# Cross-attention chain on one core: the front put in another order, with work moved between engines

## The reference, cut to what matters

```python
def L0(tgt, memory, Wq, Wk, Wv):
    q, k, v = heads(tgt @ Wq.T), heads(memory @ Wk.T), heads(memory @ Wv.T)   # 16 heads of 16
    att = softmax(q @ k.T / 4) @ v
    return tgt + att[0]
def L1(X, F):                      # X = ctx, F = L0's result
    nX, nF = layernorm(X, w1, b1), layernorm(F, w2, b2)
    attended = softmax(nF @ nX.T / 16) @ nX
    ca = gelu(attended @ fc1.T + fc1_b) @ fc2.T + fc2_b        # fc1: 256 -> 4, fc2: 4 -> 256
    nc = layernorm(ca, w3, b3)
    return nF + gamma2 * (ca + gamma1 * (softmax(nc @ nc.T / 16) @ nc))
```

## Time and profile before

| | us |
|---|---|
| median of 3 runs (lowest, highest) | 247.23 (247.22, 247.85) |
| the profiled execution's own time | 246.86 |
| its span, first to last instruction | 245.1 |
| busy: PE, DVE, ACT, POOL | 214.2, 198.0, 148.9, 124.4 |

### The profile page before, as it was taken

The page is one execution under the profiler, slowest core; times in us unless marked ns, Lnnn a source line. Parts: engine busy times, 40 slices in busy tenths (PEclk is TensorE's granted clock), DMA queues, the critical chain, the costliest instruction groups (busy, mean ns, idle before and its releaser), DMA issues.

```text
span 245.1 us, 4980 instructions
## 1 busy us (share of the span) xinstructions
PE 214.2 (87%) x1758; PEld 154.2 (63%) x1758; DVE 198.0 (81%) x391; ACT 148.9 (61%) x284; POOL 124.4 (51%) x184
## 2 busy tenths in 40 slices
PE   6989989677999999999999899999978569999750
PEld 6766548446878779697787787867645225554320
DVE  6888858899999978789899999733558958998764
ACT  2167856226778678596787968846775326666310
POOL 6000096776999999969698939200002522222220
PEclk9999999999999999999999999999999759999955
DMA  6990000242455514455243000000000022444566
GB/s 186 366 350 3 1 4 0 93 143 109 173 171 148 161 56 155 174 168 174 82 151 113 3 1 3 0 1 3 0 3 1 0 88 86 173 175 174 190 238 257
DMA packets 14712, 26.81 MB, mean 109 GB/s; under 512 B 1760, under 2 KB 1760, under 8 KB 14688
## 3 DMA queue, kind: packets, MB, share of 16 engines
q1 hardware_dynamic: 14688, 26.50, 31.2%
HBM read 18.11 MB, written 8.39 MB: 108 GB/s over the span
## 4 chain that ended last, share of the span: by engine, by line
PE 55%; DVE 28%; issue 8%; ACT 4%; POOL 2%; DVEq 0%; POOLq 0%; ACTq 0%
PE psum L981 15%; PE psum L918 7%; DVE bn L381 6%; DVE xN L401 6%; PE psum L989 5%; PE psum L873 5%; DVE nm L564 3%; PE psum L1019 3%; PE psum L1095 3%; PE psum L931 2%; DVE nmax L524 2%; PE psum L1001 2%; PE psum L946 2%; PE psum L959 2%; PE psum L888 2%
## 5 line engine op out<-in xcount | busy, mean ns | idle before, releaser
L981 PE MATMUL psum<-XT,Fall 128*128 128x256 f32 x256 | 60.9, 381 | 1.8 <-ACT Fall L763 1.8
L981 PEld LDWEIGHTS psum<-XT,Fall 128*128 128x128 f32 x256 | 46.1, 190 | 7.2 <-ACT Fall L763 2.2
L656 POOL TENSOR_SCALAR cN<-cN,nmean,rstd 128x256 f32<-128x256 f32 x64 | 38.5, 614 | 2.4 <-POOL rstd L643 2.3
L636 POOL TENSOR_TENSOR xN<-xN,tgt 128x512 f32<-128x512 f32 x28 | 35.7, 1278 | 1.6 <-DVE xN L401 1.6
L401 DVE TENSOR_SCALAR xN<-xN,bn,rstd 128x256 f32<-128x256 f32 x64 | 33.8, 571 | 0.7 <-POOL rstd L643 0.7
L786 ACT ACTIVATE PT<-psum 128x512 f32<-128x512 f32 x32 | 19.2, 599 | 24.3 <-PE psum L989 24.2
L700 POOL CAST sC<-co 128x160 bf16<-128x160 f32 x8 | 2.6, 322 | 61.6 <-DVE co L581 61.6
L793 ACT ACTIVATE E<-psum,nmax 128x256 f32<-128x256 f32 x64 | 26.8, 475 | 10.9 <-DVE nmax L524 10.9
L524 DVE TENSOR_REDUCE nmax<-psum 128x2 f32<-128x512 f32 x32 | 22.0, 686 | 13.7 <-PE psum L981 13.2
L643 POOL TENSOR_TENSOR rstd<-vps,minus_half 128x8 f32<-128x8 f32 (+1 forms) x16 | 25.0, 1564 | 15.4 <-DVE vps L392 15.3
L760 ACT ACTIVATE XT<-psum,b1s,w1s 128x512 f32<-128x512 f32 x32 | 23.1, 794 | 3.8 <-PE psum L918 3.8
(11 more groups left out here) (157 smaller groups left out, 348.5 us busy)
## 6 DMA issues: line engine op xcount, KB each, us to landing
cN<-ctx SPq DMA_DIRECT2D x32, 256.0 KB, 2.9
xN<-x SPq DMA_DIRECT2D x32, 256.0 KB, 4.2
out<-Fall SPq DMA_DIRECT2D x32, 256.0 KB, 2.3
x0T<-x0t SPq DMA_DIRECT2D x1, 256.0 KB, 2.6
wqT<-wqt SPq DMA_DIRECT2D x1, 256.0 KB, 2.9
c0T<-c0t SPq DMA_DIRECT2D x1, 256.0 KB, 3.7
wkT<-wkt SPq DMA_DIRECT2D x1, 256.0 KB, 4.8
wvT<-wvt SPq DMA_DIRECT2D x1, 256.0 KB, 5.0
```

Source lines behind the costliest of these rows:

```text
L636: pool.tensor_tensor(xN[:, b % SLOTS, :], xN[:, b % SLOTS, :], tgt2[:, :, :].rearrange("p t d -> p (t d)"), ALU.add).then_inc(y_ok, 1)
L656: pool.tensor_scalar(own, own, nmean[:, p % 4, NT * m + t:NT * m + t + 1], root_of(p, 0, m, t), ALU.add, ALU.mult)\
L981: last = pe.matmul(bank[SBANK1[b % 3]][:, t * N:(t + 1) * N], Fall[:, b, c, t * P:(t + 1) * P], XT[:, p % 4, c, m * N:(m + 1) * N], start= ...
```

## The change

It does these things, all ahead of or at the start of the loop:

- Transfers: `c0T` and `wkT` are issued by ACT, at its very start. SP issues `x0T`, `wqT`, `wvT`, then eight ctx tiles, then eight x tiles (before: two and two).
- PE's start: 3 dummy products, the mean, 2 dummy products (before: 7, then the mean).
- The keys are projected in two halves with a signal after each, into two banks, and masked half by half on DVE. The scores of the first two heads wait for the first half's two masks.
- The order behind the keys: first scores, `operand_products`, second scores, first value half, first transposes, third scores, second value half (before: products, first value half, scores, second value half, a wait for ACT's value copies, second scores).
- `output_operand` leaves DVE. POOL does the same in 17 instructions with a wait on each, after its memsets and once the algebra's `prods` are there.
- Means and variances of the first ctx tiles are made by pair (`first_variances`), and POOL takes the root and normalizes by pair. The statistics of the sixth ctx tile move behind DVE's last copy of the attention.
- All six first x tiles are added by DVE. Their normalization moves from DVE to ACT: DVE makes `shift0` = -mean/deviation, and ACT applies it with the deviation's inverse as scale (four instructions for each pair).
- `project(0)`, ACT's copy and `project_back(0)` stand before the first turn of x, with 3 and 6 dummy products around (before: 11 dummy products there, and `project(0)` in the loop).

The core of the diff:

```diff
@@ sync
-        for dst, src, arrived in ((x0T, x0t, q_in), (wqT, wqt, q_in), (c0T, c0t, k_in), (wkT, wkt, k_in),
-                                  (wvT, wvt, v_in)):
+        for dst, src, arrived in ((x0T, x0t, q_in), (wqT, wqt, q_in), (wvT, wvt, v_in)):
             sp.dma_start(dst[:, :, :], src).then_inc(arrived, 16)
...
+        for src, dst, arrived in ((c_d, cN, c_in), (x_d, xN, x_in)):
+            for b in range(SLOTS):
+                sp.dma_start(dst[:, b, :], src[b, :, :]).then_inc(arrived[b], 16)
@@ vector
-        output_operand(0)
-        dve.wait_ge(k_mm, 1)
-        for e, m in enumerate(("even", "odd")):
-            dve.tensor_scalar(kTm[:, e, :, :], tiles(bank[1]), c_(m), None, ALU.mult).then_inc(kT_ok, 1)
...
-        output_operand(1)
+        def masked(o):
+            dve.wait_ge(k_mm, o + 1)
+            for e, m in enumerate(("even", "odd")):
+                dve.tensor_scalar(kTm[:, e, o, :], bank[(1, 5)[o]][:, 0:N], c_(m), None, ALU.mult).then_inc(kT_ok, 1)
+        masked(0)
+        masked(1)
...
+        def first_variances(p):
+            dve.wait_ge(st_ok, 2 * p + 2)
...
+                if p in (1, 3):
+                    first_variances(p // 2)
...
         dve.tensor_copy(oT[:, 1, :], bank[1][:, :]).then_inc(oT_ok[1], 1)
+        statistics(2 * EARLY - 1, 0)
+        first_variances(EARLY - 1)
...
+        def shifts(p):
+            dve.wait_ge(root_ok, p + 1)
+            dve.scalar_tensor_tensor(shift0[:, p, :].rearrange("p (m t) -> p m t", t=NT),
+                                     bn[:, p, 1, :, :].rearrange("p m (t k) -> p m t k", t=NT)[:, :, :, 1], -1.0,
+                                     rstd[:, p, 1, :].rearrange("p (m t) -> p m t", t=NT), ALU.mult, ALU.mult)\
+                .then_inc(shift0_ok, 1)
+        for p in range(EARLY):
+            add(2 * p)
+            add(2 * p + 1)
+            if p >= 1:
+                shifts(p - 1)
+            statistics(2 * p, 1)
+            statistics(2 * p + 1, 1)
+            variances(p)
...
-            if b == 18:
-                output_operand(2)
@@ gpsimd
+        pool.wait_ge(alg, ALG["prods"])
+        step(pool.tensor_tensor(g12[:, :], c_("g1"), c_("g2"), ALU.mult))
+        for c in range(DC):
+            step(pool.tensor_scalar(Rt[:, c, 0:H], a5[:, c, 0:H], c_("g2", c), None, ALU.mult))
...
+        for p in range(EARLY):
+            pool.wait_ge(vps_first, 2 * p + 2)
+            pool.tensor_tensor(rstd[:, p, 0, :], vps[:, p, 0, :], minus_half[:, 0:2 * NT], ALU.pow).then_inc(root_first, 1)
+            normal(2 * p)
+            normal(2 * p + 1)
         root(0)
-        add(4)
         root(1)
-        add(5)
@@ scalar
+        for dst, src in ((c0T, c0t), (wkT, wkt)):
+            act.dma_start(dst[:, :, :], src).then_inc(k_in, 16)
...
+        evacuate(0, 0)
+        evacuate(1, 0)
+        turned_values(0)
+        evacuate(2, 0)
+        normal(0)
+        normal(1)
         evacuate(0, 1)
+        normal(2)
+        normal(3)
...
             exponentials(b)
+            if b < 2:
+                normal(b + 4)
@@ tensor
-        keep_busy(7, 4)
+        keep_busy(3, 4)
...
+        keep_busy(2, 4)
...
-        keep_busy(11, 7)
...
+        project(0)
+        keep_busy(3, 7)
+        project_back(0)
+        keep_busy(6, 7)
         turned(0, 1)
```

More of the change, by code:

```diff
@@ L548, in _ @@
             maximum(b)
+            if b == 0:
+                shifts(EARLY - 1)
             if b % 4 == 2:
@@ L800, in turned, with normal @@
             act.activation(sT[:, p % 2, :], bank[4][:, 0:NT * P].bitcast(BF16), ACT.Copy).then_inc(sT_ok[p % 2], 1)
-        for p in range(EARLY):
-            evacuate(p, 0)
+        def normal(b):
+            p, m = b // 2, b % 2
+            act.wait_ge(shift0_ok, p + 1)
+            for t in range(NT):
+                own = xN[:, b, t * D:(t + 1) * D]
+                act.activation(own, own, ACT.Identity, bias=shift0[:, p, NT * m + t:NT * m + t + 1],
+                               scale=root_of(p, 1, m, t)).then_inc(first_ok, 1)
+        evacuate(0, 0)
[4 more added lines that the diff above has]
+        normal(1)
         evacuate(0, 1)
+        normal(2)
+        normal(3)
         for b in range(B):
@@ L882, in _ @@
         last.then_inc(mean_mm, 1)
[L884 to L890 removed]
+        keep_busy(2, 4)
+        pe.wait_ge(q_in, 32)
+        for o in range(2):
+            for c in range(DC):
+                last = pe.matmul(bank[0][:, o * N:(o + 1) * N], wqT[:, c, o * P:(o + 1) * P], x0T[:, c, :],
+                                 start=c == 0, stop=c == DC - 1)
+        last.then_inc(q_mm, 1)
+        pe.wait_ge(k_in, 32)
+        for o in range(2):
+            for c in range(DC):
+                last = pe.matmul(bank[(1, 5)[o]][:, 0:N], wkT[:, c, o * P:(o + 1) * P], c0T[:, c, :],
+                                 start=c == 0, stop=c == DC - 1)
+            last.then_inc(k_mm, 1)
         def operand_products():
             pe.wait_ge(alg, ALG["prods"])
[L893 removed]
+            for dst, w, src, n in ((128, meanw, prodQ, (H + 1) ** 2), (192, scalew, prodK, U * U)):
                 for c in range(DC):
[L895 removed]
+                    last = pe.matmul(bank[6][:, dst:dst + n], w[:, :], src[:, c, :], start=c == 0, stop=c == DC - 1)
             last.then_inc(qk_mm, 1)
@@ L1156, in _ @@
                 pe.wait_ge(evac_ok, 62)
-                pe.wait_ge(alg, ALG["stR"])
+                pe.wait_ge(operand_ok, ALG["stR"])
                 for c in range(DC):
```

139 lines of the change are left out of this document (59 added, 80 removed).

## The result

The changed kernel took 249.81 us (median of 5); the median before is 247.23; the ratio of the two kernels is 1.0088 (95% interval 1.006 to 1.0116). It is slower, by more than the 0.3% that can be told apart. The profiled execution took 249.15 us, its span is 247.4 (before 246.86 and 245.1).

A forecast was written before the change was run, and what follows sets the result against it. The prediction took the kernel as bound mostly by DVE from 39 to 64 us, then by PE. Gains of 1.3 (A), 2.1 (B) and 0.4 (C), 3.8 in all, took 247.23 to 243.4 us; range 241.9 to 246.5.

The forecast's parts named there:

- part A: PE's start up to the fourth scores: 1.3 us gained (ends 2.4 and -0.3).
- part B: From the writing of tgt2 to batch 3's scores: 2.1 us gained (ends 2.9 and 0).
- First scores therefore start at Q + 3.73: PE's start: first scores follow the query projection's start by the two projections' 3.73 us.
- Q: Start of the query projection on PE, taken as 5.8 us (ends 4.7 and 7.4).
- rival 1: PE's clock comes up late at the queries, or falls before batch 0's scores: 1.86 us more, 245.2; chance 0.22.
- some 6.0: PE's work in us between first and fourth scores before; with 1.86 added, 7.6 was taken for the stretch.
- done at T + 2.7: After the first attention: POOL finishes root and four normalizations 2.7 us after tgt2, 0.3 of it for overlap with DVE's adds.
- T: The time at which tgt2 is written: 38.98 us before, about 37.6 forecast.
- Rival 2: POOL's normalizations and DVE's adds hold each other up in part B: 1.5 us later, 244.9; chance 0.15.
- the first two terms of the list: Part B's start: sixth ctx tile's statistics on DVE, ending at T - 1.1, and POOL's root, 1.0 to 1.4 us.
- Part C: The loop's middle: output_operand leaving DVE shortens PE's wait of 0.91, 0.4 us gained (ends 0 and 1.2).
- The slower rival: PE's start: transfers interleave fully and the clock stays low through both projections: 248.3 us; chance 0.06.

The follow-up runs named there:

- e9: Changed kernel with the keys' tiles issued by SP again, the sixth ctx tile's statistics back in the attention, seven dummies ahead of the mean: 244.19 us, ratio 0.985.
- e10: e3 with all seven dummy products ahead of the mean and none behind it: 243.82 us, ratio 0.985.
- e14: Kernel before with only output_operand moved from DVE to POOL: 246.97 us, ratio 0.999.
- e1: Changed kernel with six dummy products behind the mean instead of two: 247.75 us, ratio 1.001.
- e3: Changed kernel with the sixth ctx tile's statistics, and its pair's variances and root, back in the first attention's rounds: 245.34 us, ratio 0.993.
- e7: Changed kernel with six dummy products in each of PE's two waits for the third ctx pair: 248.25 us, ratio 1.004.
- e11: Changed kernel with DVE waiting ahead of its first add until POOL has made all twelve ctx normalizations: 248.8 us (1 run).
- e13: e9 with the first value half back ahead of the small products, behind the first scores: 243.45 us, ratio 0.986.
- e12: Kernel before with three dummy products, the mean, then four dummy products, instead of seven and the mean: 247.88 us, ratio 1.002.
- e8: Changed kernel with keys' tiles on SP, sixth ctx tile's statistics back in the attention, first six x tiles normalized by DVE again: 245.95 us, ratio 0.995.

## Why the prediction was wrong

Forecast 243.4, range 241.9 to 246.5; measured 249.81, above the range and with the wrong sign. Against the forecast span of 243.1 - 1.8 = 241.3 the measured one is 6.1 longer: 3.6 of it in part A, 3.2 in part B, and the end gives 0.7 back.

**Part A failed in one term and was mis-sized in two.** "First scores therefore start at Q + 3.73" took both projections at 2.4 GHz; it was Q + 6.33, as rival 1 had it for the queries, and the keys' first products were slow as well. The step that failed is the belief that the dummies had bought the clock in the kernel before for good: e9, e10 and e14 show that it comes up anywhere from just behind the mean to the keys, with the same dummies. Why it came so late here, by fewer dummies, the pause or by chance, stays open; e1's median says that filling the pause with four more dummies brings 1.8 back. With five, and a pause behind them, it was late in all four profiles that have the loads of the change as well (the change, e3, e7, e11: 3.45 to 3.78 for the queries). Q was 6.42, not 5.8; the text had weighed the interleaving and taken a value nearer the lower end "since `wqT` had needed only 2.9". And from first to fourth scores it took 8.07, not 7.6. PE's rows follow one another without a wait in this stretch, so all of it is work; the text's own "some 6.0" and 1.86 are 7.86 already, more than the 7.6 that it took. The three are 2.6, 0.6 and 0.5: `tgt2` came at 41.22 instead of 37.6. Where Q and the clock were as forecast (e13: Q = 5.64, first scores 9.61; forecast 9.5), part A's working held up to the first scores. Behind them it didn't: `tgt2` came 29.1 later, not the 28.1 forecast, with 8.01 from first to fourth scores and a wait of PE for ACT of 0.48 next.

**Part B: the step that failed is "done at T + 2.7".** It put 0.3 for the overlap of POOL's normalizations with DVE's adds. POOL was done at T + 4.3, 1.6 later. Rival 2 had this mechanism and its size (1.5), with 0.15; I held "POOL's twelve took 6.92" against it, but those twelve ran from 33.31 to 40.23, and only the last, from 39.2 on, met a pair of adds: one by one, eleven took 558 to 560 ns and that one 996, and the pair 1.75 instead of 1.29. The number that I read was an average over a stretch in which the two met once. Behind it came a loss in no rival: PE's clock fell in its waits, 1.5 us (e7). Rival 1 looked for a fall ahead of batch 0's scores, one wait too late for this execution. It does happen there too: in e11, and in e12, whose order in this stretch is that of the kernel before, where "the clock held" was read from one profile.

```profile
47.88 3.56 PE L982 MATMUL psum<-XT,Fall 128*128 128x256 f32 x8 [1.10 <-ACT Fall L763]
```

In e12 these 1.6 us cost nothing, since DVE's normalizations set the pace up to batch 3's scores (13.30 from batch 0's, before 13.31; the earlier trace rows); in e11, where ACT has them, it took 10.77 instead of 9.10.

So the changed kernel's batch 0 scores were at T + 13.45 instead of T + 10.3, though the first two terms of the list, statistics and root, were right (POOL began its normalizations at T + 0.1).

**What was right in part B:** ACT's normalizations (2.07 for four, 1.9 forecast), the shifts, which never were last, and batch 0's to batch 3's scores, forecast 9.0, measured 9.10. e8 shows their worth, 2.7 us, and e3 that the whole of part B works once the statistics stay where they were: batch 3's scores at T + 18.16, forecast T + 19.3.

**Part C:** forecast 0.4 with an end at 0; alone 0.1 (e14), which can't be told from nothing. The doubt in the text ("it also hangs on ACT") was the answer. The POOL steps cost nothing, as forecast (7.29 to 12.83).

**Chances.** The slower rival (0.06) needed Q and lost clock together past 9.6; it was 6.42 + 2.6 = 9.0, not enough alone. What made the change slower was rivals 1 and 2 at the same time, 2.6 and 1.6: together 4.2, already more than the 3.8 forecast. The clock in the waits (1.5), Q (0.6) and the order behind the keys (0.5) came on top. I had given the two together no chance of a slower kernel, and added neither's knock-on to the other. They are not independent: in a wait that POOL caused, the clock took a price of its own (e7).

**Slips in the sums.** Q = 5.0, B 2.9 and C 0.8 are 5.8 off, so the forecast's own bound was 241.4, not 241.9. T + 8.4 with 0.6 and 1.45 is T + 10.45, not T + 10.3. The page of before has 36 slices at 9 tenths, of which the first 31 stand in a row. None of these changes the outcome.

## What to carry to other kernels

A small step that is moved "into a gap" must be followed to what waits for its result: here 0.6 us of statistics, made at 39.18 instead of 28.13 (e3), moved four POOL instructions onto DVE's two-input adds, and then PE into waits in which its clock fell, 4.5 us in all. Before a price is taken for an overlap, see whether the two engines really ran side by side in the rows that it is read from. And where PE's clock rises or falls within a few microseconds of work, take runs, not one profile, for the price.
